# TensorE's order in two stages: head sums ahead of the turns of rows, turned inverses ahead of the projection of queries and keys

## The reference, cut to what matters

```python
# layer 0 mixer, first part: H = 8 heads, E = 4 states, L = 32
G  = sigmoid(einsum('ntd,hed->nhet', X, w_G) + b_G)
K  = einsum('ntc,hdc->nhtd', X, w_K);  V = einsum('ntc,hdc->nhtd', X, w_V)
A  = 1.0 - minimum(G.sum(axis=1), 1.0)            # decays, one for each state and token
gK = einsum('nhet,nhtd->netd', G, K)              # head sums
gV = einsum('nhet,nhtd->netd', G, V)
nK = scan(A, gK, init_K);  nV = scan(A, gV, init_V)   # y = a*y + x over the tokens
# layer 1 mixer: 16 heads of 16
Q, K, V = x @ WQ, x @ WK, x @ WV;  Q, K = rotate(Q), rotate(K)
R  = (Q K^T * decay) V
y  = group_norm(R, gamma, beta, nheads) @ WO
# layer 1 feed-forward
h  = silu(x @ gate) * (x @ up);  out = h @ down
```

## Time and profile before

| | |
|---|---|
| median of 3 runs | 1685.54 us (1682.33 to 1690.22) |
| profiled execution, its own time | 1682.9 us |
| its span | 1680.8 us |
| TensorE matmuls, weight loads | 1555.8 us (93%), 1332.1 us (79%) |
| VectorE, ScalarE, GpSimd | 1002.5 (60%), 619.9 (37%), 722.0 us (43%) |
| recurrence | about 10 to 220 us of the span |
| retention and SwiGLU | about 1140 us to the end |

### The profile page before, as it was taken

How to read it: one execution, slowest core, us unless ns; L and a number is a source line. 1 busy time by engine, 2 the same in 40 slices (tenths; PEclk the granted TensorE clock), 3 DMA queues, 4 the chain that set the end, 5 groups by cost and what they waited for, 6 DMA issues and landing times. The chain is left out here.

```text
span 1680.8 us, 35272 instructions
## 1 busy us (share of the span) xinstructions
PE 1555.8 (93%) x11930; PEld 1332.1 (79%) x11930; DVE 1002.5 (60%) x2533; ACT 619.9 (37%) x1870; POOL 722.0 (43%) x864
## 2 busy tenths in 40 slices
PE   8999989999999878778679999997999999999998
PEld 6777768888888646667579999985888888888887
DVE  6545437776777695995544555435565556555552
ACT  2333345555555564345421111112333333333331
POOL 3222234443443386883343333316454444544431
PEclk9999989999999999888779999999999999999999
DMA  7676610000000200003532222211000000000000
GB/s 199 122 161 123 110 34 14 14 14 14 13 13 2 67 1 1 26 27 103 181 101 67 73 74 68 74 52 38 27 29 19 28 19 28 28 19 28 22 9 13
DMA packets 91015, 86.32 MB, mean 51 GB/s; under 512 B 11632, under 2 KB 81072, under 8 KB 90512
## 3 DMA queue, kind: packets, MB, share of 16 engines
q1 hardware_dynamic: 73776, 56.63, 13.9%
q0 software_dynamic: 6480, 17.70, 3.8%
q10 hardware_dynamic: 10640, 10.48, 1.8%
HBM read 45.46 MB, written 22.02 MB: 40 GB/s over the span
## 5 line engine op out<-in xcount | busy, mean ns | idle before, releaser
L717 POOL TENSOR_TENSOR probs<-probs,rs 128x384 f32<-128x384 f32 x128 | 105.7, 826 | 199.1 <-DVE rs L895 198.0
L2124 PE MATMUL n_psS<-f_XT,wgu 128*128 128x128 f32 x1536 | 182.2, 275 | 0.9 <-ACT f_XT L2244 0.8
L2124 PEld LDWEIGHTS n_psS<-f_XT,wgu 128*128 128x128 f32 x1536 | 176.6, 192 | 1.7 <-ACT f_XT L2244 1.6
L852 ACT ACTIVATE probs<-psS,nm 128x192 f32<-128x192 f32 x256 | 105.5, 417 | 136.5 <-DVE nm L891 136.5
L1791 POOL DMA_INDIRECT XE<-token_rows,held x71 | 70.8, 997 | 165.2 <-PE e_psX L1810 149.7
L1820 PE MATMUL e_psH<-e_XT,e_W 128*128 128x128 f32 x1136 | 135.2, 278 | 0.0
L1820 PEld LDWEIGHTS e_psH<-e_XT,e_W 128*128 128x128 f32 x1136 | 132.3, 195 | 0.1
L1830 PE MATMUL e_psY<-w_experts,e_HT 128*128 x568 | 128.4, 379 | 0.0
L1861 ACT ACTIVATE e_HT<-e_psH 128x512 f32<-128x512 f32 x71 | 42.5, 598 | 214.8 <-PE e_psH L1820 214.8
L446 PE MATMUL psKV<-wkv,XT 128*128 128x384 f32 (+1 forms) x384 | 120.1, 463 | 0.8 <-ACT XT L496 0.8
L1830 PEld LDWEIGHTS e_psY<-w_experts,e_HT 128*128 128x128 f32 x568 | 105.2, 190 | 12.9
(11 more groups left out here) (294 smaller groups left out, 3450.7 us busy)
## 6 DMA issues: line engine op xcount, KB each, us to landing
KD<-KV SPq DMA_DIRECT2D x256, 66.0 KB, 2.5
expert_out<-YE ACTq DMA_DIRECT2D x35, 256.0 KB, 2.2
w_experts<-in_w SPq DMA_DIRECT2D x16, 512.0 KB, 6.3
X<-in_x SPq DMA_DIRECT2D x8, 512.0 KB, 6.6
x_turned<-XT SPq DMA_DIRECT2D x32, 128.0 KB, 2.3
XS<-x_turned SPq DMA_DIRECT2D x8, 512.0 KB, 4.1
token_rows<-o_XN SPq DMA_DIRECT2D x32, 128.0 KB, 1.7
out_x<-X SPq DMA_DIRECT2D x32, 128.0 KB, 1.7
```

Of the source, the lines that this page charges most:

```text
L717: nc.gpsimd.tensor_tensor(probs[:, b.q % 4, :, :], probs[:, b.q % 4, :, :], bc(rs[:, b.q % 2, :].unsqueeze(2), [P, 2, KEYS]), ALU.mult).th ...
L852: nc.scalar.activation(probs[:, b.q % 4, u, :], psS[b.q % 2][:, u, :], ACT.Exp, bias=nm[:, b.q % 2, u:u + 1], scale=scale, accum_out=sums[ ...
L2124: mm = pe.matmul(bank[:, m * P:(m + 1) * P], wgu[:, h, f:f + P], FT[:, h, :], start=(m == 0 and h == 0), stop=(m == HALF - 1 and h == KC - ...
```

## The change

Two blocks change places on TensorE and nothing else: the same instructions with the same waits.

```diff
@@ recurrence, TensorE's step @@
                 if has(0):
                     keys_values(Tile(i, s, 0))
+                if has(-2):
+                    sums(Tile(i, s, -2))
                 if has(1):
                     turned(Tile(i, s, 1))
-                if has(-2):
-                    sums(Tile(i, s, -2))
                 if has(0):
                     decays_turned(Tile(i, s, 0))
@@ retention_swiglu, TensorE's step @@
                     turn(Chunk(i, s, 1) if has(1) else None, three if has(-3) else None)
+                if has(-2):
+                    inverses_turned(two)
                 if has(0):
                     project_qk(new, has(-4))
-                if has(-2):
-                    inverses_turned(two)
                 if has(-3):
                     gate_up(three, 0, one if has(-1) else None)
```

## The result

| | before | after |
|---|---|---|
| median | 1685.83 us (6 runs, 1682.0 to 1690.22) | 1696.74 us (6 runs, 1695.29 to 1699.98) |
| ratio | 1 | 1.0065 [1.005, 1.0081] |
| profiled execution, its own time | 1682.9 us | 1699.05 us |
| span | 1680.8 us | 1697.0 us |

The change makes the kernel 10.9 us slower. The time lies in the predicted range, 4.2 us above the predicted one, and beyond the 0.5% that I had called the bound of no change.

The account below looks back on a forecast made before the run. TensorE's own order was taken to bound recurrence and retention's middle. Recurrence +8.4 - 3.7 = +4.7, retention's opening +2.3, middle 0: +7.0 us on 1685.5 gives 1692.5 us; range 1685 to 1699.

Parts of the forecast that it names:

- the 0.5% that I had called the bound of no change: Whole kernel: a measurement tells about 0.5% (8.4 us) from no change, so slower begins at 1694.0 us.
- What bounds, and the sign: Recurrence and retention's middle: TensorE's own order bounds both; the whole kernel gets slower, by +7.0 us.
- retention's middle: 28 middle steps of retention: no wait added, 0 us, with bounds of 3 us either way.
- The stall in the recurrence: Recurrence: only decays cover the copy of XT, TensorE stalls 0.18 plus 0.11 restart; period 6.24, +8.4 us over 29 steps.
- 0.84: Recurrence: us from the turn through ScalarE's copy to the next keys and values, 0.42 plus 0.42.
- Of 6.2 us this gives back 3.7: Recurrence: the longer period takes back 3.7 of 6.2 us of waits for GB; about 2.5 us remain.
- Retention's opening: First two retention steps with inverses: late spread makes inverses and the projection behind them wait, +2.3 us (0.6 to 3.4).
- rival 2: Recurrence: stalls bring the lower clock in one step of four, 10 us on top of 7.0: 1702 us; chance 0.07.
- 1: Recurrence: the copy of XT takes the long path, 1.00 us, period 6.40; +10.8 in all: 1696.3 us; chance 0.18.
- 3: Recurrence: copy there within 0.66 of the turn, period stays 5.95, waits shrink; -0.4 in all: 1685.1 us; chance 0.12.
- 4: Recurrence: the stall comes without the restart's 0.11, 3.2 us less; +3.8 in all: 1689.3 us; chance 0.13.
- The chance of 0.37: Whole kernel: probability given to slower by over 0.5%, summed over the forecast and its rivals.

Follow-up runs that it names:

- the split: Recurrence with four head sums, the turn, the other four sums, then the decays; retention as before; against the kernel before: ratio 0.9986, -2.0 us.
- the turn last: Recurrence in the order sums, decays, turn; retention as before; against the kernel before: ratio 1.0114, +19.0 us.
- the written-out kernel: Recurrence's swap alone, TensorE's and ScalarE's steps there written out instead of looped; against the kernel before: ratio 1.0024, +4.7 us.
- kernel pair with ScalarE's stores: Store of XT issued by ScalarE instead of SyncE, against the kernel before: ratio 0.9946 with the old order, 1.0040 with the recurrence's swap; retention as before.
- retention's half alone: Retention's swap without the recurrence's, against the kernel before: ratio 1.0014, +2.4 us.

## Why the prediction held, and where its sizes were off

- **What bounds, and the sign:** right. TensorE's order bounded both stages, the turn's cover was what went, and retention's middle had nothing to lose.
- **The stall in the recurrence:** mechanism right, shown by the split, by the turn last and by the trace. Of its size, "0.84" from turn to keys and values was the term that was mis-sized: it measured 0.93 and 1.01 in the loop and 0.85 outside. The 25 periods that touch the loop are 6.35 instead of 6.24, 2.7 us more: a price of 11.1 (183.6 - 172.5) instead of 8.4. I had the 0.84 from rows of written-out steps and put it into a loop; the written-out kernel gives 6.24 back.
- **"Of 6.2 us this gives back 3.7":** the 184.8 have 1.2 of waits in them, so 5.0 came back. The kernel pair with ScalarE's stores shows the price without this term: hardly any such wait is there, and the same order costs 11.3. The hand count behind the 3.7 is not borne out: at its own period of 6.24 it left 2.5 us of waits, and the one trace with that period has 4.9. It came out near because the real period was longer. The sum of the stage was +6.1 for a predicted +4.7.
- **Retention's opening:** both waits were there, at 1.25 and 1.89. What I left out is the clock behind the second one, 1.6 us more for the projection (3.51 - 1.88). The trace after shows +4.6, of which about 1.9 is the predicted 2.3, 1.6 this clock, and 1.0 a slow clock in an earlier step's scores (1.87 instead of 1.17) and what waits for them, which kernels without the change show too. By times the half is worth 2.4 us, its interval from 0 to 5.
- **The clock in the recurrence** (rival 2 and the Trainium skill's sentence in "TensorE: Matmul & The Clock Gate", section "PE-mode transpose"): six transposes in a row and a stall in each of 29 steps left the clock at 1.00 (the window of 130 to 200 us above). The rule, as I had applied it, gave a lower clock and fell to the row. Where the clock did fall was elsewhere, in retention's opening behind a wait of 1.89 us.
- **Rivals:** 1 was nearest in time (1696.3), though not for its reason: ScalarE was free, as the [1.57] of idle time before its copy shows. 3 and 4 are out: no copy within 0.66, and the restart's cost is there (keys and values 3.65 until the next piece, 158.55 - 154.90, instead of 3.55).
- **The sum:** 6.1 in the recurrence, 2.4 in retention's opening (by times) make 8.5 of 10.9. The rest isn't settled: the interval of the whole reaches from 8.4 to 13.7, and the position attention, untouched, was 4.5 us longer in the one trace of after than in that of before. That the time fell within the range is in part luck: the price of the stall was 2.7 us too low and what comes back 1.3 too low, and the two errors partly cancel; the clock in retention's opening, 1.6 us, stood in no term. The chance of 0.37 for slower by over 0.5% was too low by the period and this clock.

## What to carry to other kernels

Before a block is moved on a saturated engine, look at what its result starts on other engines and at which of the following blocks covers that path; the price is the path less the cover, in every step. Take the path's length from steps of the same kind, looped or written out. A longer period can hide waits for another feed, as here 5 of 11 us; once that feed is mended, the full price shows. And where a bound engine idles for a late feed, count what the feeding queue issues in a step: one store moved from the full queue to that of a less busy engine (ScalarE, 37%) gained 8 us here.

## What the runs showed of the hardware

- Ways over a semaphore were longer in a loop, where waits compare with a register's value: turn to copy 0.43 or 0.51 and copy to weights 0.50 in the loop, 0.42 and 0.43 with the steps written out. That it is the register's wait itself, and not something else of the loop, is an inference.
- In retention's opening the granted clock was 0.50 (1191 to 1194 us) behind a wait of 1.89 us and the projection took 3.51 instead of 1.88; in the recurrence before it averaged 0.71 (118.5 to 122 us) in the step behind the longest wait, 1.48 us by the matmul rows. Behind the wait of 1.25, and with 0.2 to 0.4 of idle time in each step, pieces kept their times. With matmuls in the wait the projection took 1.88.
- Two 128x128 transposes in a row between float32 matmuls of the recurrence held TensorE for 0.22 us, ahead of the sums (155.78 to 156.00 before) as behind them (160.28 to 160.50 after). In the split order the sums took 0.84 in each half, 1.68 instead of 1.74, which is the 0.05 of its shorter period; I have no cause for it.
- The length of the wait alone doesn't decide the clock. At retention's start, with the orders that this change doesn't touch, the first projection stands behind one long wait in every kernel (the trace before, then that of retention's half alone):

```profile
1146.02 0.41 PE L2092 MATMUL n_psK<-ident,n_XN 128*128 128x128 f32 x2 [3.82 <-DVE n_XN L2469]
1146.26 1.88 PE L2104 MATMUL n_psQK<-n_wqkv,n_XT 128*128 128x512 f32 x4
```

```profile
1148.95 0.41 PE L2092 MATMUL n_psK<-ident,n_XN 128*128 128x128 f32 x2 [2.15 <-DVE n_XN L2469]
1149.20 3.50 PE L2104 MATMUL n_psQK<-n_wqkv,n_XT 128*128 128x512 f32 x4
```

Behind the longer wait it ran at full speed, behind the shorter one at about half of it. What else decides is open.
